# Second stage of a normalise-and-convolve chain: a fourth buffer, products in another form, and group statistics formed one piece later

## The reference, cut to what matters

```
x = x + newton_schulz_inverse(gn(x), 5)          # stage one of the kernel
x = x + conv3x3_quantised(gn(x), w1)*scale+bias  # layer 1
x = x + conv5_diagonal(gn(x), w2)                # layer 2
x = x + conv3x3_circular(gn(x), w3)              # layer 3
def gn(v): g = groups(v); return (g - mean(g)) / sqrt(var(g) + eps)
```

## Time and profile before

| | |
|---|---|
| median of 3 runs | 3712.34 us (3697.12 to 3731.15) |
| profiled execution, its own time | 3719.76 us |
| its span, first to last instruction | 3717.7 us |
| TensorE busy over the span | 92% |
| VectorE, GpSimd, ScalarE busy | 79%, 74%, 68% |

### The profile page before, as it was taken

The page is one execution under the profiler, slowest core; times in us unless marked ns, Lnnn a source line. Parts: engine busy times, 40 slices in busy tenths (PEclk is TensorE's granted clock), DMA queues, the critical chain, the costliest instruction groups (busy, mean ns, idle before and its releaser), DMA issues. The chain is left out here.

```text
span 3717.7 us, 137014 instructions
## 1 busy us (share of the span) xinstructions
PE 3436.3 (92%) x58321; PEld 2903.0 (78%) x58321; DVE 2935.7 (79%) x6205; ACT 2514.6 (68%) x4686; POOL 2737.8 (74%) x3415
## 2 busy tenths in 40 slices
PE   7999999999999999999999994788888888888888
PEld 7999999999999999999999993344545455545445
DVE  5888888888888888888888885677777777777874
ACT  6766677777777767767777763676666666766763
POOL 6888888888888888888888874566666666656662
PEclk9999999999999999999999996899999999999998
DMA  2212112122211211212212212566666666666663
GB/s 67 69 58 58 61 56 68 61 60 64 69 59 58 69 58 58 69 58 58 69 58 58 69 42 73 118 159 153 144 167 145 147 166 147 165 143 144 157 145 87
DMA packets 317726, 347.23 MB, mean 93 GB/s; under 512 B 21568, under 2 KB 284224, under 8 KB 300736
## 3 DMA queue, kind: packets, MB, share of 16 engines
q1 hardware_dynamic: 317120, 338.47, 34.9%
HBM read 135.09 MB, written 134.22 MB: 72 GB/s over the span
## 5 line engine op out<-in xcount | busy, mean ns | idle before, releaser
L1462 PE MATMUL bank<-xn,wt 64*32 64x512 bf16 (+1 forms) x18432 | 969.6, 396 | 60.9 <-issue 33.8
L1462 PE MATMUL bank<-xn,wth 64*32 64x512 f16 (+1 forms) x6144 | 949.4, 396 | 9.5 <-issue 9.4
L1235 POOL TENSOR_TENSOR xn<-F,xn 128x512 f16<-128x512 f32 x512 | 539.3, 1092 | 349.1 <-ACT xn L1292 349.1
L487 ACT ACTIVATE P<-bank 128x512 f32<-128x512 f32 x1024 | 606.0, 607 | 266.0 <-PE bank L1010 155.0
L1462 PEld LDWEIGHTS bank<-xn,wt 64*32 64x32 bf16 (+1 forms) x18432 | 453.9, 95 | 201.8 <-issue 85.5
L1462 PE MATMUL bank<-xk,wt 64*32 64x512 f16 x9216 | 535.2, 384 | 66.3 <-issue 47.5
L1462 PE MATMUL bank<-xk,wth 64*32 64x512 f16 x3072 | 524.0, 384 | 17.3 <-issue 17.1
L1462 PEld LDWEIGHTS bank<-xn,wth 64*32 64x32 f16 (+1 forms) x6144 | 407.7, 95 | 151.8 <-issue 25.9
L1349 DVE SCALAR_TENSOR_TENSOR x<-bank,wu,x 128x512 f32<-128x512 f32 x512 | 367.6, 743 | 165.0 <-PE bank L1462 163.8
L1245 POOL TENSOR_TENSOR x<-x,X 128x512 f32<-128x512 f32 x256 | 322.3, 1277 | 207.8 <-ACT x L1306 207.4
L1306 ACT ACTIVATE x<-bank,bst,sws 128x512 f32<-128x512 f32 x256 | 189.3, 776 | 386.2 <-PE bank L1462 197.0
(11 more groups left out here) (147 smaller groups left out, 8501.3 us busy)
## 6 DMA issues: line engine op xcount, KB each, us to landing
xk<-xn SPq DMA_DIRECT2D x1024, 65.9 KB, 2.6
X<-in_x SPq DMA_DIRECT2D x64, 1024.0 KB, 4.8
x_scratch<-X SPq DMA_DIRECT2D x64, 1024.0 KB, 6.0
X<-x_scratch SPq DMA_DIRECT2D x64, 1024.0 KB, 6.3
out<-x SPq DMA_DIRECT2D x64, 1024.0 KB, 4.4
wf<-in_w SPq DMA_DIRECT2D x2, 192.0 KB, 6.9
wf<-in_w SPq DMA_DIRECT2D x1, 320.0 KB, 7.2
whf<-in_w1h SPq DMA_DIRECT2D x6, 1.0 KB, 5.8
```

The source lines that it names most:

```text
L487: nc.scalar.activation(into[:, 4 * q:4 * q + 4, :], banks[q][:, :].rearrange("p (m w) -> p m w", m=4), ACT.Copy).then_inc(sb, 1)
L1235: ins = nc.gpsimd.tensor_tensor(padded(xn[l][n % 2], 1)[:, a + 1:a + 5, L:L + H], F[l][:, a:a + 4, :], padded(xn[l][n % 2], 0)[:, a + 1:a ...
L1462: ins = nc.tensor.matmul(bank[cols_, :], w, v, start=(half == i == 0), stop=(half == 1 and i == length[l] - 1))
```

## The change

Four edits, all in the second stage.

1. The x2 images get X2 = 4 buffers; the first `raise_` of image n then waits for layer 2 of image n-4 where it waited for n-3. x3 and the stores keep 3.
2. Four small products of VectorE that were `tensor_tensor` are now `scalar_tensor_tensor` with the constant 1.0 as scalar: the same product, (a * 1.0) * b.
3. TensorE's `mean` moves from before to behind the first piece of layer 3, and `var` from behind the first to behind the second. VectorE's `deviations` moves behind the first `chunk_stats` of the step, and `normalise` from behind the second to behind the third.
4. ScalarE's `root` moves behind `quotients`.

```diff
-            THIRD = 3
-            xs = [None, x1s] + [[sb(f"x{l}_{n}", [H, NJ, H]) for n in range(k)] for l, k in ((2, THIRD), (3, THIRD))]
+            THIRD, X2 = 3, 4
+            xs = [None, x1s] + [[sb(f"x{l}_{n}", [H, NJ, H]) for n in range(k)] for l, k in ((2, X2), (3, THIRD))]
...
-                            need(act, evac[2], BPI * (n - 2))
+                            need(act, evac[2], BPI * (n - X2 + 1))
...
+                        if there(s + 1):
+                            quotients(s + 1)
                         if pair(s):
                             root(s - 1)
-                        if there(s + 1):
-                            quotients(s + 1)
...
+                    def product(out_, a, b):
+                        return nc.vector.scalar_tensor_tensor(out=out_, in0=a, scalar=1.0, in1=b, op0=ALU.mult, op1=ALU.mult)
...
-                        link.done(nc.vector.tensor_tensor(dev[:, :, :], dev[:, :, :], dev[:, :, :], ALU.mult))
+                        link.done(product(dev[:, :, :], dev[:, :, :], dev[:, :, :]))
...
-                        link.done(nc.vector.tensor_tensor(c["rb"][:, :], c["ra"][:, :], c["ra"][:, :], ALU.mult))
-                        link.wait()
-                        link.done(nc.vector.tensor_tensor(c["rb"][:, :], c["rb"][:, :], c["ve"][:, :], ALU.mult))
+                        link.done(product(c["rb"][:, :], c["ra"][:, :], c["ra"][:, :]))
+                        link.wait()
+                        link.done(product(c["rb"][:, :], c["rb"][:, :], c["ve"][:, :]))
...
-                        link.done(nc.vector.tensor_tensor(c["r"][:, :], c["ra"][:, :], c["rb"][:, :], ALU.mult))
+                        link.done(product(c["r"][:, :], c["ra"][:, :], c["rb"][:, :]))
...
                             whole_stats(s - 1)
-                            deviations(s - 1)
                         for u in range(BPI):
                             if there(s):
                                 chunk_stats(2, s, u)
-                            if u == 1 and pair(s):
+                            if u == 0 and pair(s):
+                                deviations(s - 1)
+                            if u == 2 and pair(s):
                                 normalise(s - 1)
...
-                            mean(s - 1)
                         for u in range(BPI):
                             if there(three):
                                 piece(3, three, u)
                             if u == 0 and pair(s):
+                                mean(s - 1)
+                            if u == 1 and pair(s):
+                                if there(s):
+                                    finish(1, s, 0)
                                 var(s - 1)
```

## The result

The changed kernel takes **3657.73 us** (median of 3 runs, 3657.02 to 3662.68) against 3712.34: the ratio is 0.9848, 95% interval 0.9818 to 0.9878, so 1.5% faster. The forecast was 3678, 0.9% faster, in a range of 3630 to 3720. The profiled execution went from 3719.76 to 3662.68 us.

What follows compares the result with a forecast made beforehand. TensorE was taken as the bound, idle at the means and for late code. Steady steps -29 us, last steps -5 and first 0 gave -34, so 3678 us; own range 3658 to 3700, stated range 3630 to 3720.

Steps and rivals of the forecast that it cites:

- Part one: TensorE at the means: the wait for VectorE's sums goes, 58.3 us in 56 steps, 1.04 a step.
- Part two: TensorE at the variances: new wait of 0.5 us a step, 28 us in the window, from products stalling behind GpSimd's adds.
- Part three: Normalise through copies to the next step's layer 2: exactly as before and as early, TensorE held no more often.
- Part four: TensorE's instruction blocks: arriving late, they take back a third of the 30 us saved net, 10 us.
- The clock: TensorE's granted clock: 6 us gained in the window, of at most about 12 hanging on the stops at the means.
- The sum: Steady window: -58.3 + 28 + 10 - 6 = -26 us in 56 steps; -34 on the whole profiled time.
- First and last steps: Outside the steady steps: first steps 0, within 3 us either way; last steps -5, between 0 and -12.
- rival 1: All is kept: no wait at the variances, code blocks come in time; 3632 us, chance 0.20.
- rival 2: Deviations miss the second add's border, wait at the variances 1.8 us a step; slower, 3738 us, chance 0.10.
- rival 3: Code fetch takes back everything, or TensorE's order is not what limits; only last steps gain: 3707 us, chance 0.15.

Runs made afterwards that it cites:

- e9: Changed kernel with the means alone put back ahead of layer 3: 3714 us, ratio 0.9997 to the kernel before.
- e2: Kernel before with only the moves of mean, var, deviations and normalise: 3665 us, ratio 0.986 to the kernel before.
- e1: Kernel before with the fourth x2 buffer alone: 3711 us, ratio 1.0002 to the kernel before.
- e3: Changed kernel with the four small products as tensor_tensor again: 3658 us, ratio 0.9851 to the kernel before.
- e10: Changed kernel with variances behind layer 3's third piece and normalise behind the fourth chunk: 3704 us, ratio 0.9976 to the kernel before.
- e4: Changed kernel with deviations also written to PSUM, so neither of their products reads two SBUF tensors: 3661 us, ratio 0.9848 to the kernel before.
- e11: Changed kernel storing each image in four 256 KB transfers, each once its piece is done: 3647.57 us, ratio 0.9816 to the kernel before.
- e12: Changed kernel with stores in four 256 KB transfers and deviations also in PSUM: 3655 us, ratio 0.9829 to the kernel before.
- e7: Kernel before storing only the first of 16 bands of each image: 3672 us, ratio 0.9891 to the kernel before.

## Why the prediction came out as it did

**The bound and its parts.** TensorE, with waits at the means and late code, was the right reading. e9 shows that without the move of the means there is no gain, and e2 that the moves alone bring it. That ScalarE's 174.8 us and the buffer are worth nothing was right (e1).

**Part one** said -1.04 us a step at the means: measured -1.02 (1.04 to 0.02).

**Part two** said a new wait of 0.5 us at the variances, from one unbroken burst of adds and products that stall in either form: measured 0.39, or 23.0 us in the window for 28, with L1379 at 1186 ns. Products and adds were right (e3).

**Part three failed.** It put the path to the next step "as before and as early", and said the copies "hold TensorE rarely today and will not more often". They cost 0.66 us a step, 39.0 us in the window, from 4.6. The step that was wrong was to compare the copies only with their own old times. TensorE's arrival at layer 2 was what moved: each step is 0.9 us shorter, and the copies, tied to the end of the adds through `normalise`, got less than that earlier. A wait removed from a loop shows up at the next link, and I had stopped at the first one. e10 shows that link directly: with scale and bias a chunk later, the wait for copies is 96.4 us.

**Part four failed in its sign.** It said late code takes back 10 us, a third of what is saved. In fact the stops called "issue" fell by 30 us in the window, 0.6 a step. They are 1.6 to 1.9 us a step in the three whole kernels with the means ahead of layer 3 (before, e1, e9) and 0.9 to 1.3 in the seven with the means behind its first piece and 16 copies (after, e2, e3, e4, e10, e11, e12); so this is tied to the placement and no accident of one profile. One reading is that a wait hides a late block when it falls on it, and that two shorter waits, at the variances and at the copies, meet more late blocks than one at the means: where the wait for copies is largest (e10), issue is the lowest of the kernels with whole stores, 54.6. e7 shows the first half of this, that a wait and a late block can fall together. That the two shorter waits meet more late blocks is argued, not shown.

**The clock** was sized at 6 us for the window and gave about 23: the busy time per step fell by 0.39 us, in 59 steps. The prediction gave the stops at the means the share of the lost clock that they have in the idle time, a third of 36 us. Measured, a clock of 0.97 and one of 0.99 are 36 and 12 us lost, two thirds less. This is no accident of one profile. The granted clock over the span is 0.972 to 0.981 in every recorded run of the kernel before, of e1 and of e9, and 0.983 to 0.986 in every one of the changed kernel, of e2 and of e3. TensorE's busy time for its 58321 matmuls is 3436.3 us before and 3407.0 after:

```profile
PE 3407.0 (93%) x58321; PEld 2848.5 (78%) x58321; DVE 2909.7 (79%) x6205; ACT 2514.8 (69%) x4686; POOL 2732.7 (75%) x3415
```

It is 3422.7 in e1 and 3428.3 in e9, so 16 to 29 us of the change's 55 are busy time. It is not the means as such: in e10, whose stops at the copies are long, the clock is 0.975 to 0.980 again.

**The sum** of -26 us in the window stands against 54 measured, in the 59 steps between the fifth and the 64th sums. It missed half of the gain, and came that near only by errors that partly cancel: 34 us of copies left out, against 40 us of late code on the wrong side and 17 of clock. First and last steps (0 and -5) were right: +1 and -4. The measured 3657.7 us lies at the lower edge of the forecast's own range, 3658 to 3700 (0.3 us in 62 steps either way is 19 us, so by its terms 3659 to 3697). The stated range reaches lower only to take in rival 1, whose first condition did not hold, so that the result lies well inside it is in part luck.

Of the rivals, none happened as told. Rival 1 had its condition about the products refuted (1186 ns), though its other one, that code comes in time, was nearer to the truth than the forecast's 10 us more; rival 2's missed border did not occur, as the longest wait at the variances was 1.2 us; rival 3 is excluded by the interval. The Trainium skill says in "Runtime: NRT & Kernel Launch", section "Instruction fetch mechanics", that crossing a block of code is mostly hidden. By number of blocks the traces agree, as two thirds of them cause no stop (171 of 256 before). By cost they don't: the stops are 39 to 111 us in 1200, more or less as transfers are dense or thin. What the Trainium skill says in "VectorE: DVE Perf Modes", section "Two Vector instructions with no wait between them", of the second read interface, shared with GpSimd, agrees with the runs: 1186 ns in the changed kernel, 1183 in e3, and 176 in e4, where one input is in PSUM.

## What to carry to other kernels

When an in-order engine waits for a small result from another, put one more unit of ready work in front of that wait, and then follow the result to its last consumer before pricing it: here the same 1.1 us of waiting moved to the variances and copies, and one unit more (e10) lost most of the gain. A long wait of an engine with time to spare can be worth nothing (174.8 us, e1), and removing a visible stall paid nothing (e4) because its successor, the copies, was already late. Look at the granted clock too: here it brought about a third to a half of the gain. The form with a scalar did not free a small VectorE product from GpSimd (e3); a PSUM operand did (e4).

## What the runs showed that I had not expected

The same bytes in fewer, larger transfers can cost more than they save: 8 copies instead of 16, all behind the low part, halved their issue (12 to 6.09 us), shortened the wait for them by 17 us, and raised TensorE's stops for code by 34 us. And idle time of TensorE is not additive: taking 57 us of waiting from the means lowered the stops called "issue" by 30 us, where the prediction had them rise by 10.
